# Row sums of one kv head of each unit taken on ScalarE and folded into the maxima as logarithms

## The reference

```
q, k = rope(x @ wq), rope(x @ wk);  v = x @ wv
scores = einsum('bqhd,bkhd->bhqk', q, k) / sqrt(32) + causal mask
attn = softmax(scores);  out = einsum('bhqk,bkhd->bqhd', attn, v) @ wo
x = layernorm(x + out)
x = layernorm(x + ((silu(x @ gate.T) * (x @ up.T)) @ down.T))
```

## Time and profile before

| | |
|---|---|
| median of 3 runs | 1830.34 us (1829.82 to 1830.5) |
| profiled execution | 1831.06 us, its span 1829.3 us |
| PE busy | 1782.9 us, 97% of the span |
| DVE, ACT, POOL busy | 1203.7, 710.7, 531.8 us |
| mean granted clock of TensorE | 0.997 of full speed |

### The profile page before, as it was taken

The page is one execution under the profiler, slowest core; times in us unless marked ns, Lnnn a source line. Parts: engine busy times, 40 slices in busy tenths (PEclk is TensorE's granted clock), DMA queues, the critical chain, the costliest instruction groups (busy, mean ns, idle before and its releaser), DMA issues.

```text
span 1829.3 us, 26734 instructions
## 1 busy us (share of the span) xinstructions
PE 1782.9 (97%) x10128; PEld 856.6 (47%) x10128; DVE 1203.7 (66%) x2239; ACT 710.7 (39%) x1115; POOL 531.8 (29%) x805
## 2 busy tenths in 40 slices
PE   7999999999999999999999999999999999999998
PEld 4655555455555533444444444444444444444444
DVE  7887788678778764556554445746656765667656
ACT  5354444444435444356334343341332322222221
POOL 1454546446446552221000001202311211112203
PEclk9999999999999999999999999999999999999999
DMA  9345335234324499467634354548521211222301
GB/s 272 72 119 114 65 93 145 47 79 143 76 53 128 99 225 278 162 218 265 245 129 146 122 173 174 181 162 186 153 69 53 71 64 47 77 93 89 121 12 81
DMA packets 228735, 233.34 MB, mean 128 GB/s; under 512 B 184064, under 2 KB 184576, under 8 KB 228608
## 3 DMA queue, kind: packets, MB, share of 16 engines
q1 hardware_dynamic: 227600, 231.13, 42.8%
q10 hardware_dynamic: 1008, 0.52, 0.1%
HBM read 122.81 MB, written 72.88 MB: 107 GB/s over the span
## 4 chain that ended last, share of the span: by engine, by line
PE 84%; DVE 7%; POOL 3%; issue 2%; DMA 2%; SPq 1%; ACT 1%; DVEq 0%; POOLq 0%; ACTq 0%
PE bank L1089 33%; PE bank L983 18%; PE bank L1109 14%; PE bank L1122 6%; PE bank L1034 4%; PE bank L995 3%; PE bank L1021 3%; PE bank L1049 2%; DVE down_forms L1467 1%; DVE bank L1325 1%; POOL p_tiles L1532 1%; DVE gate_blocks L1461 1%; SPq L1668 1%; POOL p_tiles L1524 1%; DMA att_parts<-att_spill 0%
## 5 line engine op out<-in xcount | busy, mean ns | idle before, releaser
L1089 PE MATMUL bank<-x_forms,weight_forms 128*128 128x512 f16 x3136 | 701.6, 379 | 10.2 <-DVE up_blocks L1451 3.9
L1089 PEld LDWEIGHTS bank<-x_forms,weight_forms 128*128 128x128 f16 x3136 | 305.4, 98 | 384.4 <-DVE gate_blocks L1451 6.6
L1182 ACT ACTIVATE p_tiles<-bank 128x512 f32<-128x512 f32 (+1 forms) x352 | 193.4, 556 | 264.8 <-PE bank L1021 260.1
L1109 PE MATMUL bank<-down_forms 128*128 128x512 f16 (+1 forms) x1168 | 258.1, 376 | 0.0
L983 PE MATMUL bank<-wq_parts,xT_parts 128*128 128x256 f16 x1536 | 219.7, 274 | 8.2 <-DVE wq_parts L1279 8.0
L1486 DVE TENSOR_TENSOR acc<-bank,acc 128x512 f32<-128x512 f32 x188 | 127.7, 687 | 124.1 <-PE bank L1109 64.9
L1325 DVE CUSTOM_DVE_ANT_0 bank<-bank,cmask 128x384 f32<-128x384 f32 (+1 forms) x256 | 157.8, 633 | 61.2 <-PE bank L995 59.6
L1524 POOL TENSOR_SCALAR_AFFINE_SELECT p_tiles<-p_tiles 128x128 f32<-128x128 f32 (+2 forms) x352 | 135.5, 393 | 211.0 <-ACT p_tiles L1182 210.6
L983 PEld LDWEIGHTS bank<-wq_parts,xT_parts 128*128 128x128 f16 x1536 | 147.0, 98 | 67.6 <-issue 16.6
L983 PE MATMUL bank<-wo_parts,att_parts 128*128 128x512 f16 x672 | 173.4, 383 | 4.1 <-DVE row L1373 2.8
L1109 PEld LDWEIGHTS bank<-down_forms 128*128 128x128 f16 x1168 | 114.3, 98 | 134.6 <-DVE down_forms L1467 0.2
(11 more groups left out here) (122 smaller groups left out, 2036.8 us busy)
## 6 DMA issues: line engine op xcount, KB each, us to landing
weight_forms_spill<-weight_forms SPq DMA_DIRECT2D x28, 896.0 KB, 4.0
weight_forms<-weight_forms_spill SPq DMA_DIRECT2D x28, 896.0 KB, 4.5
x_forms_spill<-x_parts SPq DMA_DIRECT2D x56, 256.0 KB, 2.7
w_page<-gateT SPq DMA_DIRECT2D x28, 512.0 KB, 5.4
w_page<-upT SPq DMA_DIRECT2D x28, 512.0 KB, 3.8
w_page<-downT SPq DMA_DIRECT2D x28, 512.0 KB, 4.0
att_spill<-att_made SPq DMA_DIRECT2D x64, 128.0 KB, 2.2
down_forms<-x_spill SPq DMA_DIRECT2D x16, 512.0 KB, 3.4
```

The lines of the kernel that those rows point to most:

```text
L1089: t = nc.tensor.matmul(strassen[bank_set(use)][to][:, :], w_form[:, use % 4, A_FORMS[a_form], k * P:(k + 1) * P], xF[:, :, B_FORMS[b_form] ...
L1109: t = nc.tensor.matmul(to[:, 0:cols.stop - cols.start], hid_p[place_of(r)][:, k, a, i // 2 * P:(i // 2 + 1) * P], wd_p[place_of(r)][:, c, ...
L1182: nc.scalar.activation(p32[j][:, h0:h0 + heads, :], bank[5 + m % 2][:, 0:heads * n].rearrange("p (h c) -> p h c", c=n), ACT.Exp, scale=SCO ...
```

## The change

For kv head G = 0 of each unit (`LOGGED`) the row sums are no longer taken by PE from `p_tiles`. Instead:

- `row_sum` (new, ACT): after `row_max`, each head's scores by queries in bank 3 or 4 are exponentiated in place with the negated maximum as bias, and ACT's accumulator gives the row's sum. The bank is free for `score_q` only after it. These are 11 of the 22 bank uses of a unit, 16 exponentials (4 each of 128, 256, 384 and 512 columns). The scores are taken in an order in which the two kv heads alternate.
- `ln_seed` (DVE) and 3 times `ln_exp` (ACT) and `ln_step` (DVE, 2 instructions): the logarithms of the sums, from the bits of the number and three corrections with an exponential.
- `max_parts` (DVE) subtracts the logarithms from the negated maxima and splits the result in 3 fp16 parts (`MROWS` = 3), 6 instructions where 2 stood. The second scores then give probabilities that are already divided, so for G = 0 `presum`, `sums`, `sum_turn` and `att_scale` are gone, and `att_hi` and `att_lo` read the pv bank. The next head's first `pv` waits for these two.
- `nat_lo` moves from DVE to POOL.
- For i = 0, 1 and G = 0, DVE scales the negated maxima by one more small instruction (3 per unit). The second mask tensor and its DMA are gone.
- `score_q` ranks move from `SLOT * (u - 1) - 10` to `SLOT * (u - 1) - 16`, and the maxima's chain by 4 later.

Cut to its core, the diff is:

```diff
-MROWS = 2
+MROWS = 3
+ROW_ORDER = ([0, 4], [4, 0, 2, 6], [4, 0, 1, 5, 6, 2, 3, 7], [4, 0, 1, 5, 6, 2, 3, 7])
+LOGGED = 0
+SUM_USES = [(i, h) for i, h in ROW_USES if h // REP == LOGGED]
...
-        put(VE, end + 3, .6, "nat_lo", *one, after=[("nat_hi", *one)])
+        put(PO, end + 3, .95, "nat_lo", *one, after=[("nat_hi", *one)] + ([("nat_lo", *one_back)] if r else []))
...
-        at = SLOT * (u - 1) - 10.0
+        at = SLOT * (u - 1) - 16.0
...
+            if summed:
+                k = SUM_USES.index((i, h))
+                put(SC, at + n * SLOT / NROW, ROW_HEADS[i] * (.44 + (i + 1) * P / 1200), "row_sum", u, i, h,
+                    after=[("row_max", u, i, h)] + ([("row_sum", u, *SUM_USES[k - 1])] if k else []))
...
-        put(PE, at + 3.5, 2.4 if final else 1.65, "sums", u, G, takes="T", after=[("causal", *one)] + [("presum", u, G, 1)] * (not final))
+        if G != LOGGED:
+            put(PE, at + 3.5, 2.4 if final else 1.65, "sums", u, G, takes="T", after=[("causal", *one)] + [("presum", u, G, 1)] * (not final))
...
+                    if m > 1 and ("row_sum", *rows_of[m - 2]) in rsum_n:
+                        on.wait_ge(s_rsum, rsum_n["row_sum", *rows_of[m - 2]])
...
+                elif kind == "row_sum":
+                    on.wait_ge(s_max, m + 1)
+                    on.wait_ge(s_part, PARTS * (u - 1))
+                    for h in range(ROW_HEADS[i]):
+                        t = nc.scalar.activation(scores[:, h, :], scores[:, h, :], ACT.Exp, scale=SCORE_DOWN if i < MAX_MASKS else -1.0,
+                                                 bias=mx[:, u % 2, i, h0 + h:h0 + h + 1],
+                                                 accum_out=row_sums[:, u % 2, i, (h0 + h) % REP:(h0 + h) % REP + 1])
...
+                elif kind == "ln_exp":
+                    on.wait_ge(s_ln, LN_ENDS * u + 2 * k + 1)
+                    nc.scalar.activation(ln_z, ln_y[:, :, :], ACT.Exp, scale=-1.0).then_inc(s_lnexp, 1)
...
+                elif kind == "ln_step":
+                    nc.vector.tensor_tensor(ln_z, ln_z, row_sums[:, u % 2], ALU.mult).then_inc(s_ln, 1)
+                    nc.vector.scalar_tensor_tensor(ln_y[:, :, :], ln_z, -1.0, ln_y[:, :, :], ALU.add, ALU.add).then_inc(s_ln, 1)
...
```

More of the change, by code:

```diff
@@ L395, in attention_plan @@
             ("stack", "k", b, j)] + [("exp", *keys[m - 2])] * (m > 1) + [("score_k", *keys[m - 1])] * (m > 0))
-        freed = [("pv", *last, j), ("sums", *last) if j < 2 else ("presum", *last, j - 1)] if q else []
+        freed = [("pv", *last, j)] if q else []
+        if q and last[1] != LOGGED:
+            freed.append(("sums", *last) if j < 2 else ("presum", *last, j - 1))
         put(SC, at + .5, .12 + cols / 1075, "exp", *one, after=[("score_k", *one)] + freed)
@@ L783, in block_kernel @@
         row_n = {w: n for n, (k, w) in enumerate([p for p in plan.order[PE] if p[0] == "score_q"])}
+        rows_of = list(row_n)
         rot_n = {w: n for n, (k, w) in enumerate([p for p in plan.order[VE] if p[0] == "rotate"])}
-        for engine, kind in ((PO, "rope_add"), (SC, "nat_hi"), (VE, "nat_lo"), (SY, "stack")):
+        for engine, kind in ((PO, "rope_add"), (SC, "nat_hi"), (PO, "nat_lo"), (SY, "stack")):
             assert [w for k, w in plan.order[engine] if k == kind] == list(rot_n), kind
```

181 lines of the change are left out of this document (118 added, 63 removed).

## The result

| | before | changed |
|---|---|---|
| median, 5 runs each on one chip | 1830.34 us (1829.82 to 1832.27) | 1838.0 us (1833.99 to 1843.25) |
| ratio | | 1.0039, 95% 1.0025 to 1.0054 |
| profiled execution, its span | 1831.06, 1829.3 us | 1843.25, 1841.5 us |
| PE busy, PE idle in the span | 1782.9, 46.4 us | 1779.4, 62.1 us |
| mean granted clock of TensorE | 0.997 | 0.986 |

The changed kernel is 0.4% slower. The forecast was 1817.3 us, 0.7% faster. A second measurement gave 1.0026, so the sign is certain and the size is about 5 to 8 us. The profiled execution is the longest of its five; the runs with a lower granted clock are mostly the longer ones (1833.99 us at 0.992, 1843.25 at 0.986), which is the first hint at a cause.

What follows compares the result with a forecast made beforehand. PE's own work was taken as the bound, busy 1782.9 of 1829.3 us. 1831.06 - 24.0 + 11 = 1818.1 us for the profiled execution, the median 0.7 us lower: 1817.3 us; 8 of 10 range 1803 to 1834.

Steps and rivals of the forecast that it cites:

- PE's work, -24.0: On PE in attention: one group of sums for each of 16 units, 1.50 us each, goes: 24.0 us.
- a busy PE that hasn't fallen by some 24 us: Sign against the forecast, which had PE's busy time fall to about 1759 us.
- at the full clock (granted 1.00): PE's state from 40 to 640 us before the change, busy 589.7 of 600 us.
- Added idle, 11 us: New PE idle time in attention, mostly in units 0 to 4: 11 us, bounds -5 to 30.
- The 4.6: Added PE idle from 40 to 200 us with ACT 90% full: 10.8 us, where 6.2 were before.
- ScalarE at 96% of PE's work: Units 0 to 4: ACT has 146.5 us of work against PE's 152.6, so ACT binds as much as PE.
- the 8 that I had set to refute my placing: Sign: more than 8 us of idle PE after 230 us would refute placing the new idle before 230 us.
- I take it as hidden but for unit 4: The maxima's chain after the last row maximum, 4.7 us and four handovers, is covered by PE's work except in unit 4.
- my fourth rival: Logarithms late: each unit's transpose waits for ACT steps in a full queue; at 2 us a unit, 1838 us; chance 0.09.
- I charge nothing: Start of the second stage: its x_forms loads move nearly as far as PE does, so 0 us.
- at most 325 ns: Duration of each new small DVE instruction, none wider than 32 columns; 4.6 us for a unit, 73 in all.
- 17 to 53: Fall of DVE's work in us, from nat_lo, transposes, reciprocal and product gone, less the new small instructions.

Runs made afterwards that it cites:

- The idle matmuls: Changed kernel plus 50 matmuls of 256 columns, result unread, in four places of unit 4's hole: 1832.17 us, ratio 1.0002 to the kernel before.
- the best version: Changed kernel with LN_STEPS = 1, SLOT 45, score_q at -13, no end += 4, output projections spread otherwise: 1818.32 us, ratio 0.9925 to the kernel before.

## Why the prediction was wrong

**PE's work, -24.0: right as work, within some 3 us.** Putting it back costs 20.7 us. But "a busy PE that hasn't fallen by some 24 us" was to refute me, and it fell by 3.5.

**The clock: the step that was missing.** No term of the sum had it: "at the full clock (granted 1.00)" went into the sum as something that stays. The kernel before ran at 1.00 from 40 to 640 us with short and few waits. The change makes longer ones, and matmuls behind them run at the lower level. Of the 20.5 us by which PE's remaining work grew, the windows put 15.4 to the clock in attention (18.2 less 2.8) and 1.6 in the second stage; the mean clocks of the two spans give 19.6 together. So this is the largest term of all, and 1 to 3.5 us of it are not accounted for. These are sizes of the profiled execution, the longest of its five; at the median the loss is smaller. The idle matmuls show the cause for one hole; for the others it is taken over from there.

**Added idle, 11 us: too small and put down to the wrong engine.** In attention it grew by 17.1 us:

| stretch | forecast | measured | of it |
|---|---|---|---|
| 40 to 200 us | 4.6 | 2.2 | the transpose for unit 3's maxima 2.7; ScalarE ended 0.2 of PE's waits from 40 to 640 us |
| 200 to 230, unit 4 | 4.4 | 6.0 | row maxima 3.6, the maxima's DMA 1.9, the sums' bank 0.9 |
| 230 to 640 | 2 | 4.3 | GpSimd's masking 4.8 (was 2.4), the maxima's DMA 1.2, a bank behind the rotation 1.1 |
| 640 to the first product | 0 | 4.0 | ScalarE's exponentials 3.0 (was 1.3), the sums' bank in unit 15 2.8, the maxima's DMA 2.0 |
| 0 to 40 | 0 | 0.6 | |

The 4.6 is also added up wrong: the four ScalarE times over 0.90 leave 11.4 us of idle PE, not 10.8, so it should have been 5.2. The place of the worst hole was right, with the reason from the order. The reason for the rest, ScalarE at 96% of PE's work, was wrong: it was busy 68% from 40 to 200 us, in part since I had added up instructions that overlap, and with 75 us less on it nothing changed. After 230 us there are 8.3 us new, past the 8 that I had set to refute my placing. Most of what came between 230 and 640 us is one wait, and no maximum is in it (GpSimd, then PE):

```profile
470.70 2.28 POOL L1611 TENSOR_SCALAR_AFFINE_SELECT p_tiles<-p_tiles 128x128 f32<-128x128 f32 x1
473.03 1.61 PE L1075 MATMUL bank<-p_tiles,v 128*32 128x512 f32 x8 [3.58 <-POOL p_tiles L1611]
```

The mask of one head takes 2.28 us where the two before it take 0.29 and 0.30, while VectorE runs two instructions with two SBUF inputs, from 471.01 to 471.68 and from 471.61 to 472.81 us. That this is the same holding the other way round is argued, not tested.

**"I take it as hidden but for unit 4": wrong, the step that failed among those I priced.** I had the chain at 4.7 us and four handovers. VectorE's timeline at unit 15 shows what it is in a shared queue (some rows left out):

```profile
675.32 0.17 DVE L1390 TENSOR_SCALAR ln_sums<-row_sums 128x16 f32<-128x16 int32 x1
677.14 0.69 DVE L1486 SCALAR_TENSOR_TENSOR x_parts<-row,x_parts 128x512 f16<-128x512 f32 x1 [1.66 <-ACT x_parts L1255]
677.75 0.17 DVE L1395 TENSOR_TENSOR max_parts<-max_parts,row_sums 128x16 f32<-128x16 f32 x1
...
679.42 0.69 DVE L1452 SCALAR_TENSOR_TENSOR row<-bank,row 128x512 f32<-128x512 f32 x1 [1.28 <-DMA row<-x]
...
683.78 0.19 DVE L1414 TENSOR_TENSOR max_parts<-row_max,max_parts 128x32 f16<-128x32 f32 x1
```

From the last row maximum to the last part it takes 8.5 us, before 0.5. The steps themselves are 0.17 us each; the time goes to what stands between them in an engine that works in order, layer norm pieces that wait for ScalarE and for a DMA. PE's wait at this place reads:

```profile
685.84 0.38 PE L1045 MATMUL bank<-idH,max_parts 128*24 128x128 f16 x4 [2.80 <-DVE over_sum L1426]
```

The parts are ready at 683.97 us, so the chain makes 0.9 of the 2.80 us; the rest is the same queue once more, in which VectorE comes to the sums' bank (L1426) only behind further layer norm pieces. Without the corrections the kernel is 0.42% faster. That was my fourth rival, 1838 us, and the time came out there. I gave it 0.09 because I looked at the sum of the steps and at PE's cover in the mean unit. But that the number fits is chance: there are no 2 us in every unit, but a few large waits, about half of what was lost is the clock's, and some waits have nothing to do with the logarithms.

**"I charge nothing" for the second stage's start: the term was 0, and 4.0 us of new idle time stand in front of it.** The loads of x_forms did move with PE, but to later: the last of the first set is issued at 708.16 us, 11.2 later, and the first product starts 12.0 later. SP's queue carries both the x_forms loads and the maxima's rows of the last unit, one behind the other. SP's issues:

```profile
688.89 1.24 SPq L1755 DMA_TRANSPOSE x_forms<-x_forms_spill  x1
690.18 2.04 SPq L1698 DMA_DIRECT2D q_stack<-max_rows  x3
```

VectorE had copied these rows by 687.77 us, so they waited 2.4 us for the queue. Before, the same rows went out at 668.69 us, 21.5 earlier, while the first load of x_forms was issued at 632.4 before and 639.1 after. By this mark the changed kernel was 6.7 us behind near 640 us; the other 5.3 of the 12.0 us were lost from there to the first product. How much of these the late maxima caused, and how much the queue, wasn't tested apart.

**VectorE's instructions, "at most 325 ns": too low** where GpSimd adds: 441 ns for two columns. In busy time this is small, but in the chain it isn't: 2.27 us in one link were behind the longest wait for maxima, and without the long presums the kernel is 0.60% faster. VectorE fell by 30 us, inside 17 to 53. GpSimd fell by 16.5, where I had it gain 10.

**Why unit 4.** The filler for PE's waits is projections, and the early units eat it: by unit 4's first `score_k` 26 q pieces are used where 24.1 were, by unit 5's 28.2 for 28. With the first head's sums gone, which were work for PE that waited for little, the same projections must cover more. This is counted from the order; no run tested it by itself. In the best version, with other slots and one correction, PE is busy 9.75 and 10.00 of 10 us at 210 and 220 us, at clock 1.00.

## What to carry to other kernels

Where TensorE hardly ever waits and runs at its upper clock throughout, price each new wait twice: for itself, and for the matmuls behind it at the lower level. Taking work off the bound engine pays in full only if the filler still covers its waits, so a removed filler and a lengthened chain should be ordered anew together, and the old kernel must get the same tuning before the edit is credited (here 0.36% of 0.75%). A chain of short steps across two busy engines costs what stands between the steps in their queues, and how long another engine holds them up, not the steps' sum.
